# A pre-norm block with linear attention and a mixture of experts: weights folded through the attention, carried router columns, experts with stationary weights

## The chip, the core and the metric

The kernel runs on one core of one Trainium2 chip. The metric is the device time in microseconds (us) of one execution; the median of three runs is given. All arrays are fp32. TensorE is called PE, VectorE DVE, ScalarE ACT, GpSimd POOL and SyncE SP; each is a queue that runs its instructions strictly in the order written, so an instruction that waits on a semaphore holds up all that stand behind it on its engine.

## The reference, cut to what matters

```python
# x: (4, 1024, 128); 16 heads of 8; 16 experts of 128 -> 2*128 -> 128; shared FFN of 512
n = layernorm(x)
q, k = l2norm_per_head(n @ Wq + bq), l2norm_per_head(n @ Wk + bk)
v = n @ Wv + bv
out = (q @ k.T / S ** sigmoid(m)) @ v          # no softmax, per batch and head
x = x + out @ Wo + bo
h = layernorm(x)
logits = h @ router_w.T                        # 16 experts, top 1
s = sigmoid(top logit)                         # of the chosen expert, else 0
gate, up = split((s * h) @ gate_up[e])
expert = (up * silu(gate)) @ down[e]
shared = silu(h @ shared_gate_w.T) * (h @ shared_up_w.T) @ shared_down_w.T
return x + shared + expert
```

## The kernel before, in words

The 4096 rows are 32 tiles of 128 rows, taken as 8 quads of 4 tiles (`NQ`, `Q`); two quads are one batch (`QB`). Since there is no softmax, attention of a batch is q times a 128x128 matrix: the sum over rows of v^T k, masked to the heads' blocks and multiplied by Wo.

Every engine's program is a list of calls written out by hand, one call per helper and quad (or per shared chunk `n`, 4 per quad, or per expert group `g`, 4 slots of 128 rows each, 12 groups). The lists are different on the five queues and semaphores tie them together; nothing is reordered while it runs.

**Stage one, attention and routing, quads in turn.** PE: `project` (x against q, k and v weights, 384 columns, L1096), `v_by_k` (L1105), `fold_wo` (L1114), `turn_q` (transposes, L1122), `attend` (the bias as a matmul, L1129, x by the identity, L1130, q by the folded matrix, L1135), `turn_h` (L1143), `route` (h against 16 router columns, L1152), `count_before` (how many earlier rows chose each expert). DVE: `stats` (L721, L724), `take` (scales and biases the projection, L758), `head_sums` (L766), `inv_norms` (L771), `h_scales` (L743, L744), `choose` and `place` (the chosen expert of each row and its row in the sorted array, L791 to L811; their temporaries lie in PSUM). ACT: squares, roots, PSUM copies, `norm_h`. POOL: `scale_q` and `scale_v` (L319), `hT_lo` (L329), `count` (L336) and `scatter` (L345): one indirect DMA per tile writes its 128 rows of h, with score and row number, to their places in `x_slots` in DRAM, at most two in flight.

**Shared FFN.** h is split in a high part (rounded to fp32r) and a remainder, `hT_lo`, and each product of it is three fp32r matmuls of 512 columns: `gate_up_shared` (6 matmuls, L1181 to L1183), `silu_shared` on ACT, `act_shared` on DVE (L843), `down_shared` (L1203). 32 chunks; they fill PE between the other work and make the tail.

**Stage two, experts.** When all 32 scatters have landed and `table` (first row and expert of each of the 48 slots, by `slot_rows` and `take_table` on DVE) is there, SP loads the slots, 4 DMAs per group (`load`, L248), 12 groups in turn. Per group: `turn_rows` on PE (L1215), `rows_copy` on ACT (L528), `gate_up_experts` (rows stationary, weights of the expert moving, 4 matmuls of 256 columns, L1226), `score_tanh` on ACT and `score` on DVE, `gate` (four ACT instructions, L536), `gated` (four on DVE, L868), `turn_act` (four transposes of the activations, L1234) and `turned_act` (L877), `down_experts` (L1245), `take_y` (L545), and `send` on POOL (L354): one indirect DMA per slot back to `y_back`, at most three in flight.

**Tail.** When all 48 have landed, SP brings `y_back` in 8 DMAs (L254), `add_shared` (L849) and `add_experts` (L855) on DVE add up, and 8 DMAs write `out` (SP and ACT queues in turn).

Of the kernel before, what the change touches and what calls it, by code (L numbers as in the profile page):

```python
# [7 lines left out]
ALU = mybir.AluOpType  # L8
ACT = mybir.ActivationFunctionType
AX = mybir.AxisListType  # L10
# [8 lines left out]
def build_block(nc, S, x, x_t, w_in, b_in, Wo, bo, m_col_in, router_t, gate_up, down, shared_gate, shared_up,  # L19
                shared_down, out):  # L20
# [6 lines left out]
    _, E, F2 = gate_up.shape  # L27
    F = F2 // 2
# [8 lines left out]
    QKV = 3 * D  # L37
    W = D + 2
    QRING = 2
    RING = 3  # L40
    EPS = 1e-5
    YRING = 12
# [9 lines left out]
    with ExitStack() as ctx:  # L52
# [6 lines left out]
        xres = sb("xres", [P, NT, D])  # L59
# [4 lines left out]
        st1 = sb("st1", [P, NT, 6])  # L64
        mv1 = sb("mv1", [P, NT, 2])
        rs1 = sb("rs1", [P, NT])
        nm2 = sb("nm2", [P, NT])
        st2 = sb("st2", [P, NT, 6])
        mv2 = sb("mv2", [P, NT, 2])
        rs2 = sb("rs2", [P, NT])  # L70
        w_o = sb("w_o", [P, D])
# [11 lines left out]
        rwT = sb("rwT", [P, E])  # L83
# [7 lines left out]
        s_act = sb("s_act", [P, 2, 512])  # L91

        place_of = sb("place_of", [P, Q, E])
        near = sb("near", [P, Q])
        hot = sb("hot", [P, NQ, E, Q])
        incl = sb("incl", [P, 2, E, Q], BF16)
        run_mask = sb("run_mask", [P, E, Q])
# [19 lines left out]
        with ExitStack() as attention:  # L117
            def sb_a(name, shape, dt=F32):
                return attention.enter_context(nc.sbuf_tensor(name, shape, dt))

            qkv = sb_a("qkv", [P, QRING, Q, QKV])
            sq = sb_a("sq", [P, Q, 2 * D])
            xT = sb_a("xT", [P, T])
            qT = sb_a("qT", [P, RING, Q * P])
            ss = sb_a("ss", [P, 2, Q, 2 * HEADS])
            rn = sb_a("rn", [P, 2, Q, 2 * HEADS])
            vkm = sb_a("vkm", [P, 2, D])
            wb = sb_a("wb", [P, 2, D])
            w_qkv = sb_a("w_qkv", [P, D + QKV])
            b_qkv = sb_a("b_qkv", [P, QKV])  # L130
            w_c = sb_a("w_c", [P, QKV])
# [3 lines left out]
            zeros = sb_a("zeros", [P, E, W])  # L135
            w_sh = sb_a("w_sh", [P, 2, SF])
            bo_in = sb_a("bo_in", [2, D])
            bo_top = sb_a("bo_top", [2, D], F32R)
            bo_two = sb_a("bo_two", [P, Q, D], F32R)
            two_col = sb_a("two_col", [2, 1])  # L140
            ones_r = sb_a("ones_r", [P, P], F32R)
# [1330 lines left out]
```

## Time and profile before

| | |
|---|---|
| median of 3 runs | 213.24 us (212.55 to 214.74) |
| the profiled execution | 212.35 us |
| its span, first to last instruction | 210.6 us |
| PE busy | 185.7 us, 88% |
| DVE busy | 137.5 us, 65% |
| POOL busy | 111.8 us, 53% |
| ACT busy | 103.1 us, 49% |
| mean DMA rate over the span | 102 GB/s |

The span is what the trace covers; 1.75 us of the execution's own time lie around it. Busy shares are means over very different stages, so they are read with the strips of the page (40 slices of 5.3 us) and with the timelines. A matmul of fp32 is two PE instructions in the trace; their recorded durations overlap, so work is better measured from start to start.

### The profile page before, as it was taken

The page shows a single profiled execution, that of the slowest core. Times are in us where ns is not written, and L with a number is a line of the kernel's source. Part 1 is how long each engine was busy: PE and PEld are TensorE (multiplying, and loading weights), DVE is VectorE, ACT ScalarE, POOL GpSimd, SP SyncE. Part 2 cuts the span into 40 slices and gives each one's busy share as a digit, 9 for nine tenths or more (in the row PEclk, how much of TensorE's full clock was granted, in tenths as well). Part 3 has the DMA queues.
Part 4 walks back from the last instruction along what each step waited for, and adds up shares of the span by engine and source line. Part 5 has one row for each costly group of instructions (what it writes and reads, how often), then busy time and mean ns, then how long its engine had stood idle before and what let it go on. Part 6 is the DMA issues. An engine that isn't in the chain of part 4 may idle for free.

```text
span 210.6 us, 3716 instructions
## 1 busy us (share of the span) xinstructions
PE 185.7 (88%) x1110; PEld 152.0 (72%) x1110; DVE 137.5 (65%) x430; ACT 103.1 (49%) x234; POOL 111.8 (53%) x142
## 2 busy tenths in 40 slices
PE   0797698988989699889779999999999999979992
PEld 0344566766668477778568999889999889869882
DVE  4789999999999979667443455454545233237553
ACT  3434474967564798943323666565634322312320
POOL 7003405348779786757800177767777767750000
PEclk9999999999999999999999999999999999999998
DMA  6999993001100011111134456511111100048143
GB/s 171 302 390 269 174 413 134 2 0 38 40 30 25 26 38 41 51 40 51 41 85 106 114 136 154 143 43 43 42 40 38 50 31 0 0 135 311 56 165 133
DMA packets 17606, 21.58 MB, mean 102 GB/s; under 512 B 3224, under 2 KB 11679, under 8 KB 17332
## 3 DMA queue, kind: packets, MB, share of 16 engines
q1 hardware_dynamic: 13872, 15.73, 26.3%
q0 software_dynamic: 2560, 4.24, 6.1%
q10 hardware_dynamic: 1156, 1.39, 1.9%
q8 instruction: 9, 0.15, 0.3%
q14 instruction: 9, 0.07, 0.1%
HBM read 13.95 MB, written 8.44 MB: 106 GB/s over the span
## 4 chain that ended last, share of the span: by engine, by line
PE 35%; DVE 31%; DMA 12%; POOL 10%; issue 8%; ACT 2%; POOLq 1%; ACTq 0%; DVEq 0%
PE quad_banks L1226 8%; DVE qkv L758 7%; DMA y_back<-yg,xg 7%; PE bank L1203 7%; POOL y_back L354 7%; DVE ss L766 4%; DVE st L721 4%; PE quad_banks L1181 3%; PE bank L1245 3%; PE quad_banks L1183 3%; PE quad_banks L1182 3%; DMA x_slots<-h_rows,pos 3%; POOL x_slots L345 2%; PE bank L1215 2%; PE quad_banks L1096 2%
## 5 line engine op out<-in xcount | busy, mean ns | idle before, releaser
L354 POOL DMA_INDIRECT y_back<-yg,xg x48 | 47.0, 979 | 30.9 <-ACT yg L545 15.2
L843 DVE TENSOR_TENSOR s_act<-quad_banks,sg_act 128x512 f32<-128x512 f32 x32 | 22.1, 689 | 28.9 <-PE bank L1203 16.6
L517 ACT ACTIVATE sg_act<-quad_banks 128x512 f32<-128x512 f32 x32 | 19.1, 598 | 44.5 <-PE quad_banks L1183 44.4
L345 POOL DMA_INDIRECT x_slots<-h_rows,pos x32 | 31.6, 988 | 11.8 <-issue 6.9
L1203 PEld LDWEIGHTS bank<-sdT,s_act 128*128 128x128 f32 x256 | 31.8, 191 | 1.8
L1203 PE MATMUL bank<-sdT,s_act 128*128 128x128 f32 x256 | 32.8, 276 | 0.0
L319 POOL TENSOR_TENSOR qkv<-qkv,rn 128x512 f32<-128x512 f32 x16 | 17.1, 1081 | 26.6 <-DVE rn L771 26.5
L1096 PE MATMUL quad_banks<-w_c,xT 128*128 128x384 f32 x64 | 25.0, 525 | 2.1 <-DVE qkv L758 1.3
L1226 PE MATMUL quad_banks<-w_gu,xgT 128*128 x96 | 22.9, 381 | 0.8 <-ACT xgT L528 0.8
L868 DVE SCALAR_TENSOR_TENSOR e_act<-quad_banks,esc,eg_act 128x128 f32<-128x128 f32 x48 | 13.5, 344 | 10.6 <-ACT eg_act L536 10.6
L1096 PEld LDWEIGHTS quad_banks<-w_c,xT 128*128 128x128 f32 x64 | 11.9, 204 | 11.0 <-issue 3.6
L1226 PEld LDWEIGHTS quad_banks<-w_gu,xgT 128*128 128x128 f32 x96 | 17.3, 190 | 2.9 <-issue 1.0
L536 ACT ACTIVATE eg_act<-quad_banks,esc 128x128 f32<-128x128 f32 x48 | 13.7, 371 | 9.3 <-PE quad_banks L1226 8.6
L758 DVE SCALAR_TENSOR_TENSOR qkv<-quad_banks,rs,b_qkv 128x384 f32<-128x384 f32 x32 | 17.6, 601 | 0.5 <-PE quad_banks L1096 0.5
L1181 PE MATMUL quad_banks<-hT,sgT 128*128 128x512 f32 x32 | 14.8, 462 | 3.3 <-DVE s_act L843 1.9
L877 DVE COPY e_actT<-bank 128x512 f32<-128x512 f32 x12 | 8.3, 690 | 13.0 <-PE bank L1234 13.0
L721 DVE BATCH_NORM_STATS2 st<-xres 128x6 f32<-128x128 f32 x64 | 13.7, 277 | 0.3 <-DMA xres<-L_attn_x 0.3
L473 ACT ACTIVATE h_rows<-xres,nm,rs 128x128 f32<-128x128 f32 x32 | 13.2, 484 | 1.0 <-DVE nm L744 1.0
L1245 PE MATMUL bank<-w_dn,e_actT 128*128 x96 | 12.7, 275 | 0.0
L1183 PE MATMUL quad_banks<-hT,sgT 128*128 128x512 f32 x32 | 12.7, 395 | 0.0
L1182 PE MATMUL quad_banks<-hT,suT 128*128 128x512 f32 x32 | 12.7, 395 | 0.0
L1245 PEld LDWEIGHTS bank<-w_dn,e_actT 128*128 128x128 f32 x96 | 12.3, 191 | 0.5
(141 smaller groups left out, 348.0 us busy)
## 6 DMA issues: line engine op xcount, KB each, us to landing
xg<-x_slots SPq DMA_DIRECT2D x48, 65.0 KB, 1.9
xT<-x_t SPq DMA_DIRECT2D x8, 256.0 KB, 7.1
xres<-L_attn_x SPq DMA_DIRECT2D x8, 256.0 KB, 7.2
w_gu<-gate_up SPq DMA_DIRECT2D x1, 2048.0 KB, 14.4
h_rows<-y_back SPq DMA_DIRECT2D x8, 256.0 KB, 5.4
x_slots<-zeros SPq DMA_DIRECT2D x1, 1040.0 KB, 16.4
w_dn<-down SPq DMA_DIRECT2D x1, 1024.0 KB, 16.4
out<-xres SPq DMA_DIRECT2D x4, 256.0 KB, 2.0
```

Source lines behind the costliest of these rows:

```text
L345: g.indirect_dma_start(out=x_slots, out_offset=bass.IndirectOffsetOnAxis(ap=pos[:, t:t + 1], axis=0), in_=h_rows[:, t, :], in_offset=None) ...
L354: nc.gpsimd.indirect_dma_start(out=y_back, out_offset=bass.IndirectOffsetOnAxis(ap=xg[:, n, D + 1:D + 2].bitcast(I32), axis=0), in_=yg[:, ...
L517: a.activation(sg_act[:, n % 2], pair[:, 2 * (n % 2)], ACT.Silu).then_inc(s_silu, 1)
L721: last = v.bn_stats(st[:, t, :], xres[:, t, :])
L758: last = v.scalar_tensor_tensor(out=qkv[:, c % QRING, j, :], in0=pair[:, j, 0:QKV], scalar=rs1[:, t:t + 1], in1=b_qkv[:], op0=ALU.mult, op ...
L843: v.tensor_tensor(s_act[:, n % 2], pair[:, 2 * (n % 2) + 1], sg_act[:, n % 2], ALU.mult).then_inc(s_act_rdy, 1)
L1096: last = te.matmul(pair[:, j, 0:QKV], xT[:, P * (Q * c + j):P * (Q * c + j + 1)], w_c[:], start=True, stop=True)
L1181: te.matmul(to, lhs[:, 0], rhs[:, 0], start=True, stop=False)
L1182: te.matmul(to, lhs[:, 0], rhs[:, 1], start=False, stop=False)
L1203: last = te.matmul(Y_BANK[c][:, here], s_act[:, n % 2, here], sdT[:, D * k:D * k + D], start=(k == 0 and j == 0), stop=(k == KC - 1 and j ...
L1226: mm = te.matmul(gate_up_banks(g % 2)[:, j, :], xgT[:, g % 2, P * j:P * j + P], gu_cols[:, bass.ds(held[g][j] * 2, F2)], start=True, stop= ...
L1245: mm = te.matmul(ps_yg[:, here], e_actT[:, g % 2, here], dn_cols[:, bass.ds(cols[j], D)], start=True, stop=True)
```

## The change

1. No product for v. `project` multiplies by q, k and the 16 router columns only (272 columns). `gram` multiplies the scaled k by the raw rows of x with two more columns (128 + 2); `turn_g` and `v_of_g` bring Wv and bv in afterwards, once per batch. `scale_k` takes the place of `scale_v`, and its factor takes one more DVE multiply (`scale_inv`).
2. Router logits are carried: x's part is kept by `keep` (from the projection), the attention's part comes as 16 more columns of `attend` (`wo_x` has 144 columns), `sum_logits` adds the two. `route` is gone. The temporaries of the choice (`lg`, `far`, `offs`, `rank`) lie in SBUF, and the one helper is cut in ten calls with their own places in the list. `scatter` waits also for the score and for `norm_h`.
3. `attend` transposes x with bo added by ACT (`bias_x`) instead of the bias matmul and the identity product, in two halves per quad.
4. Statistics of two tiles are taken by one instruction over interleaved rows, so that even and odd elements are the two tiles; the aggregation is gone.
5. Experts: DVE multiplies the loaded rows by the score (`scale_rows`), ACT copies each slot's gate/up weights to a fixed place (`take_weights`), PE holds the weights stationary with the rows moving (8 matmuls of 128 columns), so that activations come out transposed: `turn_act` and `turned_act` are gone, `gate` and `gated` are one instruction each.
6. Remainders `hT_lo` are all on POOL, six of the eight now ahead of the last scatters.
7. All lists are written anew.

```diff
-            def attend(c, after=None):
...
-                te.matmul(ps_qy[:], ones_r[:], bo_two[:].rearrange("p j d -> p (j d)"), start=True, stop=False)
-                te.matmul(ps_qy[:], ident[:], xres[:, Q * c:Q * c + Q, :].rearrange("p j d -> p (j d)"), start=False,
-                          stop=False)
+            def attend(c, h, after=None):
...
+                for j in (0, 1):
+                    te.matmul(ps_y[:, YW * j:YW * j + D], xT_b[:, c % XRING, P * (2 * h + j):P * (2 * h + j + 1)], ident[:],
+                              start=(j == 0), stop=False, is_transpose=True, skip_group_check=True)
...
+            def gram(c, after=None):
...
+                    last = te.matmul(ps_v[:, 0:W], qk[:, c % QRING, j, D:QK], xres[:, Q * c + j, :],
+                                     start=(h == 0 and j == 0), stop=(h == QB - 1 and j == Q - 1))
...
+            def gate_up_experts(g, after=None):
+                pe.wait_ge(w_rdy, g + 1)
+                pe.wait_ge(xgT_sb, g + 1)
+                free(after)
+                for half in (0, 1):
+                    for j in range(Q):
+                        here = slice(P * j, P * j + P)
+                        mm = te.matmul(pair[:, 2 * (g % 2) + half, here], w_now[:, (g * Q + j) % WRING, F * half:F * half + F],
+                                       xgT[:, g % 2, here], start=True, stop=True)
...
+            def take_weights(g):
...
+                for j in range(Q):
+                    last = a.copy(w_now[:, (g * Q + j) % WRING], gu_cols[:, bass.ds(first[j] * 2, F2)])
...
             def stats(c, rows, st, done):
+                for n in (0, 1):
+                    last = v.bn_stats(st[:, 2 * c + n, :], by_two(rows, Q * c + 2 * n))
...
+            def below_top(c):
+                need(("top", c))
+                mark(("below", c), v.tensor_tensor(far[:, c % 2], lg[:, c % 2], top[:, quad(c)].unsqueeze(2).broadcast_to([P, Q, E]), ALU.is_lt))
...
+            def scale_rows(g):
+                dve.wait_ge(esc_rdy, g + 1)
...
+                v.tensor_tensor(rows, rows, esc[:, here].unsqueeze(2).broadcast_to([P, Q, D]), ALU.mult).then_inc(xg_rdy, 1)
```

ACT's new list around the first expert groups:

```diff
+            score_tanh(0)
+            silu_shared(11)
+            hT_copy(7)
+            score_tanh(1)
+            hT_hi(7)
+            silu_shared(12)
+            rows_copy(0)
+            score_tanh(2)
+            silu_shared(13)
+            score_tanh(3)
+            gate(0)
+            rows_copy(1)
+            score_tanh(4)
+            take_weights(2)
+            take_y(0)
+            rows_copy(2)
+            score_tanh(5)
+            score_tanh(6)
+            gate(1)
+            take_weights(3)
+            score_tanh(7)
+            rows_copy(3)
+            score_tanh(8)
+            take_y(1)
+            rows_copy(4)
+            score_tanh(9)
+            gate(2)
+            take_weights(4)
+            score_tanh(10)
+            score_tanh(11)
+            gate(3)
+            rows_copy(5)
+            take_y(2)
```

DVE's new list in the same place:

```diff
+            scale_rows(3)
+            gated(0)
...
+            scale_rows(6)
+            gated(1)
...
+            scale_rows(9)
+            gated(2)
...
+            scale_rows(11)
+            gated(3)
```

POOL's new list from the first scatter on, with runs of one call drawn together: scatter 0 to 3, count 1, `hT_lo(0)`, scatter 4 and 5, `scale_k(4)`, scatter 6 and 7, `scale_k(5)`, `scale_q(4)`, `scale_q(5)`, count 2, `hT_lo(1)`, scatter 8, count 3, scatter 9 to 12, `scale_k(6)`, scatter 13 and 14, `scale_q(6)`, count 4, scatter 15, `scale_k(7)`, `scale_q(7)`, scatter 16, count 5, scatter 17 and 18, `hT_lo(2)` to `hT_lo(4)`, scatter 19 and 20, count 6, scatter 21 and 22, `hT_lo(5)`, scatter 23 to 26, count 7, scatter 27 to 31, `hT_lo(6)`, `hT_lo(7)`, then the 48 sends. PE's new list puts 13 `gate_up_shared` and 9 `down_shared` ahead of `turn_rows(0)` (before: 10 and 8).

## Rows read from the trace of the kernel before

**Rows 1.** The page's strips: busy tenths of two engines in 40 slices.
```profile
PE   0797698988989699889779999999999999979992
DVE  4789999999999979667443455454545233237553
```

**Rows 2.** DVE groups by line: busy us, mean ns, idle before and releaser.
```profile
L758 DVE SCALAR_TENSOR_TENSOR qkv<-quad_banks,rs,b_qkv 128x384 f32<-128x384 f32 x32 | 17.6, 601 | 0.5 <-PE quad_banks L1096 0.5
L721 DVE BATCH_NORM_STATS2 st<-xres 128x6 f32<-128x128 f32 x64 | 13.7, 277 | 0.3 <-DMA xres<-L_attn_x 0.3
...
L766 DVE TENSOR_REDUCE ss<-sq 128x128 f32<-128x1024 f32 x8 | 9.6, 1200 | 0.2 <-ACT sq L489 0.2
...
L771 DVE RECIPROCAL rn<-rn 128x128 f32<-128x128 f32 x8 | 7.5, 934 | 0.0
L724 DVE BATCH_NORM_AGGREGATE mv<-st 128x2 f32<-128x6 f32 x64 | 6.1, 157 | 0.6
```

**Rows 3.** DVE timeline, stage one: start us, us, line, what.
```profile
11.04 1.14 DVE L758 SCALAR_TENSOR_TENSOR qkv<-quad_banks,rs,b_qkv 128x384 f32<-128x384 f32 x2 [0.18 <-PE quad_banks L1096]
...
45.58 0.16 DVE L811 TENSOR_TENSOR pos<-bank,near 128x4 int32<-128x4 f32 x1
```

**Rows 4.** POOL timeline, stage one: first and last scatters, and two others.
```profile
46.67 1.19 POOL L345 DMA_INDIRECT x_slots<-h_rows,pos  x1 [0.63 <-issue]
...
55.92 2.12 POOL L319 TENSOR_TENSOR qkv<-qkv,rn 128x512 f32<-128x512 f32 x2
...
60.49 1.29 POOL L329 TENSOR_TENSOR hT<-hT_full,hT 128x512 fp32r<-128x512 f32 x1
...
79.96 0.98 POOL L345 DMA_INDIRECT x_slots<-h_rows,pos  x1 [0.58 <-DVE pos L811]
...
101.95 0.96 POOL L345 DMA_INDIRECT x_slots<-h_rows,pos  x1 [0.31 <-issue]
```

**Rows 5.** PE groups by line, of products that go or shrink.
```profile
L1096 PE MATMUL quad_banks<-w_c,xT 128*128 128x384 f32 x64 | 25.0, 525 | 2.1 <-DVE qkv L758 1.3 <-ACT w_c L451 0.7
...
L1130 PE MATMUL bank<-xres,ident 128*128 128x512 f32 x16 | 8.2, 591 | 0.0
L1152 PE MATMUL bank<-rwT,hT_full 128*128 128x16 f32 x64 | 8.0, 257 | 0.2 <-ACT hT_full L479 0.2
```

**Rows 6.** The chain that ended last, expert stage: start us, us, what.
```profile
118.98 1.73 PE quad_banks L1226 x8
120.71 0.44 PE bank L1234 x4
```

**Rows 7.** PE timeline: two shared chunks in a row, and the first expert rows.
```profile
97.29 0.48 PE L1181 MATMUL quad_banks<-hT,sgT 128*128 128x512 f32 x1
...
99.59 0.48 PE L1181 MATMUL quad_banks<-hT,sgT 128*128 128x512 f32 x1
...
109.34 0.60 PE L1215 MATMUL bank<-ident,xg 128*128 128x128 f32 x4
```

**Rows 8.** SP's queue: the 48 slot loads, from the first issue to the last.
```profile
105.79 30.36 SPq L248 DMA_DIRECT2D xg<-x_slots  x48
```

**Rows 9.** ACT group, a copy of 512 columns in the expert stage.
```profile
L528 ACT COPY xgT<-bank 128x512 f32<-128x512 f32 x12 | 7.2, 597 | 8.6 <-PE bank L1215 8.6
```

**Rows 10.** DVE instructions with two inputs in SBUF: ns min/median/max; one of them in time.
```profile
L744 DVE SCALAR_TENSOR_TENSOR nm<-mv,rs x8: 161/162/1572, 35.7 to 85.9; 128x4 f32<-128x4 f32 x8
...
L784 DVE TENSOR_TENSOR suT<-w_sh,suT x1: 2265/2265/2265, 64.6 to 64.6; 128x512 fp32r<-128x512 f32 x1
...
57.47 0.59 DVE L744 SCALAR_TENSOR_TENSOR nm<-mv,rs 128x4 f32<-128x4 f32 x1
```

**Rows 11.** The end: the first and last send, and DVE's last instruction.
```profile
120.39 1.01 POOL L354 DMA_INDIRECT y_back<-yg,xg  x1 [14.94 <-ACT yg L545]
...
183.67 0.98 POOL L354 DMA_INDIRECT y_back<-yg,xg  x1 [0.30 <-issue]
...
207.43 0.69 DVE L855 TENSOR_TENSOR xres<-xres,h_rows 128x512 f32<-128x512 f32 x1
```

More of the change, by code:

```diff
@@ L408, in _ @@
             scatter(25)
-            count(6)
             scatter(26)
@@ L927, in _ @@
+            x_stats(5)
+            keep(2)
+            x_stats(6)
+            inv_norms(2)
+            take(3, 0)
+            gram_out(0)
+            x_stats(7)
+            scale_inv(2)
+            take(3, 1)
+            mask_vk(0)
+            keep(3)
+            weights_lo(0)
+            weights_lo(1)
+            head_sums(3)
+            take(4, 0)
+            x_scales(5)
+            inv_norms(3)
+            sum_logits(0)
             x1_stats(0)
-            x_scales(5)
-            head_sums(3)
@@ L930, in _ @@
-            x_stats(6)
-            inv_norms(3)
+            top_logit(0)
+            scale_inv(3)
+            below_top(0)
             h_scales(0)
+            places(0)
+            nearest(0)
+            choose(0)
+            run_count(0)
+            score_row(0)
+            keep(4)
+            h_shift(0)
+            take(4, 1)
             x1_stats(1)
-            take(4, 0)
-            take(4, 1)
-            x_stats(7)
+            add_base(0)
+            own_only(0)
+            ranks(0)
@@ L937, in _ @@
             h_scales(1)
-            mask_vk(1)
-            weights_lo(0)
-            head_sums(4)
-            choose(0)
+            put(0)
+            sum_logits(1)
+            gram_out(1)
+            h_shift(1)
+            top_logit(1)
+            below_top(1)
+            places(1)
+            nearest(1)
+            take(5, 0)
+            head_sums(4)
+            mask_vk(1)
+            choose(1)
+            run_count(1)
+            take(5, 1)
+            add_base(1)
+            own_only(1)
@@ L942, in _ @@
+            keep(5)
+            ranks(1)
+            put(1)
+            score_row(1)
+            x_scales(6)
+            x_scales(7)
+            head_sums(5)
             inv_norms(4)
-            place(0)
-            take(5, 0)
-            x_scales(6)
-            take(5, 1)
+            scale_inv(4)
+            inv_norms(5)
+            sum_logits(2)
             x1_stats(2)
-            choose(1)
+            top_logit(2)
+            below_top(2)
             h_scales(2)
-            head_sums(5)
@@ L951, in _ @@
-            place(1)
+            score_row(2)
+            h_shift(2)
+            scale_inv(5)
             take(6, 0)
-            inv_norms(5)
+            take(6, 1)
+            places(2)
+            nearest(2)
+            sum_logits(3)
             x1_stats(3)
-            x_scales(7)
-            take(6, 1)
-            h_scales(3)
-            choose(2)
-            head_sums(6)
-            mask_vk(2)
-            place(2)
+            choose(2)
+            top_logit(3)
+            run_count(2)
@@ L962, in _ @@
+            gram_out(2)
+            below_top(3)
+            add_base(2)
+            own_only(2)
+            ranks(2)
+            put(2)
+            places(3)
+            h_scales(3)
+            h_shift(3)
+            nearest(3)
+            mask_vk(2)
+            choose(3)
+            run_count(3)
+            head_sums(6)
+            add_base(3)
+            own_only(3)
+            ranks(3)
+            put(3)
+            keep(6)
+            score_row(3)
             inv_norms(6)
+            scale_inv(6)
```

1451 lines of the change are left out of this document (816 added, 635 removed).

## The prediction, on record before the result was seen

> **What bounds the kernel now.** I read the strips first [rows 1]: DVE is full in the first third, PE from the middle to the end. So it is two kernels. In stage one a quad costs what its chain on DVE costs [rows 2, 3]; in stage two PE runs without a gap from the first expert rows at 109.34 [rows 7]. Then I read the queues that no busy share shows. POOL issues its first scatter at 46.67 and its last at 101.95 [rows 4]; the slot loads start at 105.79, once all scatters have landed [rows 8], and the first rows reach PE at 109.34, 6.4 us after the last scatter's end (102.9). SP needs 30.36 us for the 48 loads [rows 8]: 2.53 us per group. Nobody waits for that now, since no engine's list takes a group's rows much before it needs them. The sends run from 120.39 to 183.67, 1.28 us apart once they are steady [rows 11]. The end is PE at 206.6 and 4 us of DVE and output behind it.
>
> I call T the time when group 0's rows are in. Before, T is 109.3 and the rest takes 210.6 - 109.3 = 101.3 us. I forecast the two separately.
>
> **What PE saves, and why most of it is not on the path.** `project` has 272 columns instead of 384: 32 matmuls, about a fifth to a quarter of 25.0 us, 6 us [rows 5]. `route` goes: 7 us of 8.0 recorded. Identity product and bias product become four transposes per quad: 5 us (from 8.2, with the bias). All that is 18 us less in stage one, where DVE and POOL set the pace, and where PE already waits. It only lets chunks of the shared FFN move ahead. `turn_act` goes from stage two: 12 x 0.44 [rows 6] = 5.3 us. Stationary weights cost 8 matmuls of 128 columns, by the 0.44 for four half-price transposes 1.78 us, against 1.73: +0.6 in all.
>
> **DVE in stage one.** The first position is written at 45.74 [rows 3]. By then the list holds five quads of `take`: a tile costs 601 ns recorded, 0.52 from start to start, and 128 columns less save 0.13 at the slope that the 128-column ones share: 20 x 0.13 = 2.6. Ten quad statistics lose their aggregation and half of their instructions: 1.19 to 0.70 each, 5.0. One `head_sums` (1.12) and one `inv_norms` (0.85) move behind it: 2.0 [rows 2]. Added are `keep`, `scale_inv`, the subtraction in `x_scales`, the copy of `wo_x`, one weight remainder and the sum of logits: 3.6. The first `take` comes later: ACT now does `bias_x(0)`, which waits for the last of its loads, and `bias_x(1)` before `wc_copy`, and the weights' product waits for the bias load; I put it at 12.6 against 11.04 [rows 3], +1.6. Sum 45.7 - 9.6 + 3.6 + 1.6 = 41.3, with 1 us of waits on the longer chain from `gram` to `wb` 42.3. The choice itself keeps its count. Carried down the list, DVE alone would place the last quad near 87, against 96 now.
>
> **POOL in stage one.** This is the step that I think decides. Behind the first scatter POOL has 31 steps of 1.28 and a last 0.96, 8 scalings at 1.0, six `hT_lo` at 1.2 and seven counts at 0.1 (durations by [rows 4], less the gap that they fill): 39.7 + 1.0 + 8.0 + 7.2 + 0.7 = 56.6. In before two of those remainders stood there and there were 4 us of idle time. Scatters also wait for the landing of the one two before: the last sixteen took (101.95 - 79.96) / 15 = 1.47 each [rows 4]; I take 3 us for that, 1 for late inputs. 42.6 + 56.6 + 4 = 103.2. So the nine microseconds that DVE gains end on POOL, and the last scatter ends where it ended. Bounds: no wait at all, 98.5 to 99; waits as dense as now over all scatters, 106.
>
> **A price for the port.** The route's temporaries move from PSUM to SBUF, so that some eleven DVE instructions per quad (sum, comparison, places, choice, scan, own, position, score, `scale_inv`, shift, subtraction) read two SBUF tensors. Such instructions exist now: the shift L744, with 161 ns as a rule, took 1572 once, and 590 at 57.47, ending at 58.06 where POOL's scaling from 55.92 ends (58.04); the weight remainder L784 took 2265, beside `hT_lo` [rows 10, 4]. So DVE waits for a POOL operation that is under way. There are 24 of POOL's in stage one, each 1.1 to 1.3 us. Before the first position I count two or three such meetings, 1.5 us: last scatter 104.7, T = 104.7 + 6.4 = 111.1. Bounds 0 and 5 us.
> The Trainium skill (SBUF — State Buffer, Who interferes with whom) says that GpSimd and a DVE instruction with two SBUF inputs take turns on one port, the later one blocked for the whole instruction; the trace agrees in these three rows. Were every one of the 24 met half way, by that rule DVE would lose some 9 to 13 us; that is a rival below.
>
> **Stage two.** PE's work from T on: 12 groups at 0.44 + 1.78 + 0.89 (four down products, twice the four transposes) = 3.11 make 37.3; a gate/up and a down chunk together take 99.59 - 97.29 = 2.30 [rows 7], 19 pairs and four more downs 47.2: 84.5. Before it was 94.2 by the same count, and ran in 97.3. But the new lists read the loads ahead: ACT has `score_tanh(3)` before `gate(0)`, (6) before `gate(1)`, (9) before `gate(2)`, (11) before `gate(3)`, and DVE `scale_rows` of the same groups before `gated`. Each waits for its group's four loads, and these come every 2.53 us [rows 8], so group 11's at T + 27.5. Behind that: tanh, score, scaled rows, `gated(3)` 1.7, so that `down_experts(3)` starts at T + 29.2. Until then PE can do 6 `turn_rows`, 5 `gate_up_experts`, 3 `down_experts`, one gate/up and three down chunks, 18.3 us: it idles for 10.9 us, though shared chunks are there, since its list has none in that place. Left behind it are 84.5 - 18.3 = 66.2: PE ends at T + 95.4, with 1.5 for ACT (four weight copies and a register load per group, 1.3 to 1.5 us by half of the 597 ns [rows 9]; up to `gate(8)` ACT has 14.7 and PE 15.2) at T + 96.9. The last output is one DVE sum shorter: 3.2. So T + 100.1, against T + 101.3 now. If the loads did not bind it would be T + 1.5 + 84.5 + 2 + 3.2 = T + 91.
> Sends: the first at T + 12; group 2 is taken only behind `gate(3)`, at T + 29.3, and from there ten groups at 5.14 end at T + 80.7. Results come back 5 to 11 us later; `add_experts(0)`, with `act_shared(27)` behind it, fits at T + 86, just when PE wants it. It costs nothing as long as PE is that late; without PE's gap the sends would end the kernel 1 to 2 us earlier than this.
>
> **Sum.** 111.1 + 100.1 = 211.2 of span, 212.9 with the 1.75 around it, against 212.35 of the profiled execution: +0.6. That execution lies 0.9 under the median of 213.24, which would make it 213.8; I keep 212.8, since each of my prices for POOL's waits stands above its lower bound: no change that can be measured. (About 1% is what a measurement of this kernel can tell: below 211.1 is faster, over 215.4 slower.)
>
> **Rivals.**
> - *Faster, 29%.* Either POOL's queue is not full (landing waits hidden under the scalings, no port waits before the first position): last scatter at 100 to 101, T near 107, 107 + 100.1 + 1.75 = 208.8; or the loads come faster than now, since nothing else uses the rings then, or fall less in ACT's way: each 10% of their 2.53 is 2.8 us, and without that gap at all and T as forecast it is 111.1 + 91 + 1.75 = 203.9, where the sends (T + 12 + 61.7 + 18) hold it at 204.6. For it: the same instructions, 0.5 us apart at the start of the burst. Against it: the 30.36 us is measured with the same queue and list. 204.5 to 210.5.
> - *Slower, 27%.* The port. If DVE meets most of POOL's 24 operations, with 9 to 13 us of waits, it no longer has the 9 us in hand: `put(7)` falls at 99 to 103 and the four last scatters behind it end at 105 to 108, T = 112 to 114.5, 214 to 216.5; and where POOL is full at the same time and waits for late scalings, both add, 216 to 220. It decides from about 9 us of such waits. For it, three of some ten such instructions of now that are not scans were hit; against it, none of the eight scans, which also read two.
> - *The statistics or the port-free parts cost more than counted, so the redesign does nothing at all*, 2%: same.
> - The forecast's own case, 42%: 210.6 to 215.8.
>
> **How the numbers follow.** Faster 0.29 and 0.05 of the forecast's own: 0.34. Slower 0.27 and 0.02: 0.29. Same 0.37. The range reaches from 205.5 to 219, and leaves a tenth at each side.
>
> **What would show it.** POOL without gaps between the first and the last scatter, the last ending at 102 to 106; DVE done with the last position well ahead of scatter 28. PE's busy share falling to about 60% for 28 us behind T, `score_tanh` and `scale_rows` waiting on the slot loads, `down_experts(3)` at T + 29. PE work near 20 us less and idle time near 20 us more. DVE's `below_top` and its like at 230 ns as a rule, with some over 1 us. I am wrong if T lies under 107 (POOL's count is wrong), if the loads take under 22 us, or if DVE still places a quad every 9 us.

## The result, and the profile after

The changed kernel takes 230.45 us (median of 4 runs, 228.5 to 231.02) against 213.65 of the kernel before in the same job: ratio 1.077, 95% interval 1.068 to 1.086. It is slower, outside the range that ended at 219, and past the slower rival's 216 to 220. The profiled execution spans 229.2 us, 18.0 more than the 211.2 of my sum. Of these, 11.1 lie ahead of T (122.2 instead of 111.1) and 6.9 behind it (107.0 instead of 100.1).

The strips of the page, busy tenths and granted clock in 40 slices, answer to [rows 1].
```profile
PE   0364859959548969998896786879999999994394
...
DVE  3239789999998798568734634632231422240591
...
PEclk9999779997995997999999999999999999999589
```
PE is full only from two thirds on, has a hole just before the end, and its clock falls to half of full speed for parts of the first half. Before, the windows from 20 to 110 show a granted clock of 1.00.

**The start.** ACT's and DVE's timelines (start, us, what; in brackets the idle time before it and who ended it) answer to [rows 3].
```profile
8.87 0.29 ACT L506 ACTIVATE m_tmp<-m_col,zero_col 128x1 f32<-128x1 f32 x1 [4.76 <-DMA m_col<-m_of_column]
...
12.84 0.47 ACT L515 COPY w_c<-quad_banks 128x400 f32<-128x400 f32 x1
```
```profile
15.69 0.88 DVE L902 SCALAR_TENSOR_TENSOR qk<-quad_banks,rs,b_all 128x256 f32<-128x256 f32 x2 [1.85 <-PE quad_banks L1425]
...
48.04 0.16 DVE L1005 TENSOR_TENSOR pos<-rank,near 128x4 int32<-128x4 f32 x1
```
The load of m, a column of 128 numbers, was first on ACT's queue and is now third: it lands 7.1 us after its issue instead of 3.5, and ACT waits 4.76 us for it. The copy of the weights stands behind it in ACT's list. The first `take` is at 15.69, not at 12.6.

**DVE between the first and the last position.** Busy us of PE, PEld, DVE, ACT and POOL in that stretch, then the clock: before, and after.
```profile
45.60:95.80 50.20, 44.61 (x277) 34.95 (x276) 43.37 (x157) 33.89 (x70) 38.58 (x43) 1.00 0.11 36
```
```profile
48.00:107.80 59.80, 48.01 (x273) 39.53 (x271) 50.95 (x156) 45.63 (x96) 42.73 (x46) 0.89 0.09 29
```
DVE has as many instructions as before, 156 against 157, and is busy 7.6 us longer. Its groups in that stretch (count, busy us, mean ns, idle before) say where most of it is:
```profile
L964 DVE SCALAR_TENSOR_TENSOR far<-far,place_of 128x64 f32<-128x64 f32 x7 | 3.8, 547 | 0.1
...
L952 DVE TENSOR_TENSOR lg<-x,kept 128x64 f32<-128x64 f32 x7 | 3.2, 464 | 0.1
...
L960 DVE TENSOR_TENSOR far<-lg,top 128x64 f32<-128x64 f32 x7 | 2.9, 420 | 0.2
```
The same 64 columns, with an operand in PSUM, took 233 ns before. These means hide single long ones. Three of them, each with what GpSimd runs at the time:
```profile
53.80 1.81 DVE L1005 TENSOR_TENSOR pos<-rank,near 128x4 int32<-128x4 f32 x1
54.32 1.26 POOL L352 TENSOR_TENSOR hT<-hT_full,hT 128x512 fp32r<-128x512 f32 x1
63.03 2.46 DVE L964 SCALAR_TENSOR_TENSOR far<-far,place_of 128x64 f32<-128x64 f32 x1
62.27 3.13 POOL L342 TENSOR_TENSOR qk<-qk,rn 128x512 f32<-128x512 f32 x3
85.44 1.61 DVE L960 TENSOR_TENSOR far<-lg,top 128x64 f32<-128x64 f32 x1
84.85 2.11 POOL L342 TENSOR_TENSOR qk<-qk,rn 128x512 f32<-128x512 f32 x2
```
Each ends within 0.1 us of the end of GpSimd's instruction, or of the last in a row of them (55.61 and 55.58, 65.49 and 65.40, 87.05 and 86.96). There are nine such cases up to the last position, two of them ahead of the first, and together they took 9.8 us more than such instructions take otherwise (0.16 or 0.23 us). In the kernel before there were three, of 3.4 us.

**POOL**, its first and last scatter, for [rows 4], and SP's slot loads, for [rows 8]:
```profile
49.12 1.18 POOL L370 DMA_INDIRECT x_slots<-h_rows,pos  x1 [3.17 <-DVE pos L1005]
...
116.34 0.96 POOL L370 DMA_INDIRECT x_slots<-h_rows,pos  x1 [1.14 <-DMA x_slots<-h_rows,pos]
```
```profile
118.85 28.73 SPq L271 DMA_DIRECT2D xg<-x_slots  x48
```
**Stage two.** ACT's waits between 120 and 152 (total, times, longest), and the product that I had named:
```profile
ACT half_tanh L606 <- DMA xg<-x_slots: 16.1, 11, 2.7
```
```profile
151.01 1.15 PE L1570 MATMUL bank<-w_dn,e_act 128*128 x8 [1.69 <-DVE e_act L1081]
```
`down_experts(3)` starts at T + 28.8. This part came as forecast.

**The sends and the tail** answer to [rows 11].
```profile
203.69 0.98 POOL L378 DMA_INDIRECT y_back<-hT_full,xg  x1 [0.30 <-issue]
207.44 0.97 POOL L378 DMA_INDIRECT y_back<-hT_full,xg  x1 [2.76 <-DMA y_back<-hT_full,xg]
208.72 0.98 POOL L378 DMA_INDIRECT y_back<-hT_full,xg  x1 [0.30 <-issue]
```
```profile
214.16 0.69 DVE L1061 TENSOR_TENSOR hT_full<-x,h_rows 128x512 f32<-128x512 f32 x1 [8.34 <-DMA h_rows<-y_back]
214.77 0.68 DVE L1037 TENSOR_TENSOR s_act<-quad_banks,sg_act 128x512 f32<-128x512 f32 x1
...
226.02 0.69 DVE L1052 TENSOR_TENSOR hT_full<-bank,x 128x512 f32<-128x512 f32 x1 [2.25 <-PE bank L1537]
```
```profile
PE quad_banks L1512 <- DVE s_act L1037: 6.6, 1, 6.6
```
The last send ends at 209.7, T + 87.5. `add_experts(0)` waits for what it brings, `act_shared(27)` stands behind it in DVE's list, and PE waits 6.6 us for that. Before, the last send ended 25.9 us ahead of the kernel's end, 21.9 us ahead of PE's, and nobody waited for it.

### The profile page after: what moved, and what is told of

Read it like the earlier page. It is cut to its first block, busy times and chain, and to the rows that moved or that the text cites. A ratio compares the mean times of both kernels' runs of the same rounds, so it can differ in the third digit from the quotient of the medians.

```text
span 229.2 us, 3735 instructions
## 1 busy us (share of the span) xinstructions
PE 179.8 (78%) x1120; PEld 154.2 (67%) x1120; DVE 132.3 (58%) x341; ACT 120.7 (53%) x268; POOL 111.7 (49%) x142
## 4 chain that ended last, share of the span: by engine, by line
PE 29%; DVE 18%; DMA 13%; POOL 13%; issue 13%; SPq 10%; ACT 2%; ACTq 1%; POOLq 0%; DVEq 0%
SPq L271 8%; POOL y_back L378 6%; PE quad_banks L1425 6%; DMA x_slots<-h_rows,pos 6%; PE bank L1537 4%; PE quad_banks L1557 4%; POOL x_slots L370 4%; DMA wo_all<-wo_in 3%; PE bank L1570 3%; DVE qk L902 3%; PE quad_banks L1512 2%; DMA y_back<-hT_full,xg 2%; PE quad_banks L1514 2%; PE quad_banks L1513 2%; DVE st L866 2%
## 5 line engine op out<-in xcount | busy, mean ns | idle before, releaser
L378 POOL DMA_INDIRECT y_back<-hT_full,xg x48 | 47.3, 985 | 35.4 <-ACT hT_full L640 15.6
L342 POOL TENSOR_TENSOR qk<-qk,rn 128x512 f32<-128x512 f32 x16 | 17.1, 1077 | 31.2 <-DVE rn L922 28.4
L1425 PE MATMUL quad_banks<-w_c,xT 128*128 128x272 f32 x64 | 22.5, 504 | 6.8 <-ACT w_c L515 5.7
L1557 PE MATMUL quad_banks<-xgT,w_now 128*128 128x128 f32 x192 | 23.3, 276 | 1.7 <-DVE s_act L1037 1.1
L1557 PEld LDWEIGHTS quad_banks<-xgT,w_now 128*128 128x128 f32 x192 | 22.3, 192 | 2.4 <-issue 2.3
L1425 PEld LDWEIGHTS quad_banks<-w_c,xT 128*128 128x128 f32 x64 | 15.0, 249 | 10.9 <-ACT w_c L515 6.0
L902 DVE SCALAR_TENSOR_TENSOR qk<-quad_banks,rs,b_all 128x256 f32<-128x256 f32 x32 | 13.8, 474 | 6.4 <-PE quad_banks L1425 6.3
L622 ACT COPY w_now<-w_gu 128x256 f32 x48 | 15.7, 408 | 0.8 <-issue 0.8
L1570 PE MATMUL bank<-w_dn,e_act 128*128 x96 | 13.1, 279 | 3.5 <-DVE e_act L1081 3.2
L1570 PEld LDWEIGHTS bank<-w_dn,e_act 128*128 128x128 f32 x96 | 11.8, 191 | 4.4 <-issue 4.1
L546 ACT ACTIVATE h_rows<-x,nm,rs 128x128 f32<-128x128 f32 x32 | 13.2, 483 | 1.7 <-DVE nm L888 1.6
```

Of the source, the lines that this page charges most:

```text
L378: g.indirect_dma_start(out=y_back, out_offset=bass.IndirectOffsetOnAxis(ap=xg[:, n, D + 1:D + 2].bitcast(I32), axis=0), in_=yg[:, n // Q % ...
L902: last = v.scalar_tensor_tensor(out=qk[:, c % QRING, j, :], in0=pair[:, j, 0:QK], scalar=rs1[:, t:t + 1], in1=b_all[:, 0:QK], op0=ALU.mult ...
L1425: last = te.matmul(pair[:, j, 0:PROJ], xT[:, P * (Q * c + j):P * (Q * c + j + 1)], w_c[:, 0:PROJ], start=True, stop=True)
L1557: mm = te.matmul(pair[:, 2 * (g % 2) + half, here], w_now[:, (g * Q + j) % WRING, F * half:F * half + F], xgT[:, g % 2, here], start=True, ...
L1570: mm = te.matmul(E_BANK[g][:, here], e_act[:, g % 2, here], dn_cols[:, bass.ds(cols[j], D)], start=True, stop=True)
```

## Experiments

My theory from these rows: the redesign's arithmetic does what it should, and five orders of the lists that came with it, together with the port that DVE shares with GpSimd, make it slower. The main rival: PE's clock and the port, which no order mends. Ratios are to the kernel before in the same job (median 214.4 us for e1 to e4, 214.8 for e5 to e8, 213.0 for e9 to e12), in brackets their 95% intervals; the changed kernel's is 1.077 [1.068 to 1.086].

One trace per run also has its spread. e1_jit, e2_sends and e7_adds leave the lists ahead of T as they are in the changed kernel, and over these four traces the first scatter starts at 47.40 to 49.12, the last at 112.99 to 116.34, and T is 118.8 to 122.2. A difference ahead of T is read against that.

### e1_jit: stage two's reads in time
```
-score_tanh(2) .. score_tanh(11) ahead of gate(0), gate(1), gate(2), gate(3)
+t3 y0 r2 g1 w3 t4 r3 t5 y1 r4 g2 w4 t6 g3 r5 y2 w5 t7 ... (t score_tanh, g gate, w take_weights)
 and DVE: scale_rows(2) and (3) around gated(0), ... scale_rows(9) behind gated(6)
```

> The changed kernel, with only the calls of score_tanh, score and scale_rows moved back in ACT's and DVE's lists, so that each stands about two groups ahead of its use and no gate or gated stands behind a far later group's load. Theory (the pace of the slot loads holds ACT and DVE, and so PE, for 29 us behind the first rows): down_experts(3) starts at T + 18 to 21 instead of T + 28.8, the last send ends 6 to 8 us earlier, the time falls by 6 to 9 us to 221 to 224. Rival (PE waits there for the weight copies or for its own turn_rows, whatever the order of the scores): down_experts(3) moves by less than 3 us and the time by less than 2.

225.32 us, 1.055 [1.042 to 1.068], just over my 221 to 224; the interval only touches that of the changed kernel. ACT's waits for the loads fall from 16.1 to 4.1 us, and `down_experts(3)` comes at T + 22.0 instead of T + 28.8 (T + 18 to 21 expected). But PE still waits 6.9 us for `act_shared(27)`: the last send ends at 202.4, T + 80.9, and PE, now earlier, meets it again. So the wait behind T costs some 5 us here, less than the 10.9 that I took PE to idle.

### e2_sends: the sends in order
```
 send_one(10)
+send_one(11)
 send_one(12)
 send_one(13)
-send_one(11)
-send_one(16)
 send_one(14)
 ...
-send_one(43)   (it stood behind 45, now behind 42)
```

> The changed kernel with the 48 sends in the order of their slots instead of 12, 13, 11, 16, 14, 15 and so on. Each send waits for the landing of the one three slots before, so out of order some wait for a send issued just before. Theory (that order is why 40 sends take 58.2 us, 1.46 each, against 1.28): 1.28 to 1.32 each, the last send 4 to 6 us earlier, and since DVE waits for the results with the last chunks behind it the time falls by as much, to 225 to 227. Rival (the landings themselves are slower than before, or ACT hands the groups over late): under 1.5 us.

224.39 us, 1.051 [1.039 to 1.063]. The last four sends:
```profile
195.96 0.98 POOL L378 DMA_INDIRECT y_back<-hT_full,xg  x1 [0.30 <-issue]
197.24 0.98 POOL L378 DMA_INDIRECT y_back<-hT_full,xg  x1 [0.30 <-issue]
198.52 0.98 POOL L378 DMA_INDIRECT y_back<-hT_full,xg  x1 [0.30 <-issue]
199.81 0.98 POOL L378 DMA_INDIRECT y_back<-hT_full,xg  x1 [0.30 <-issue]
```
A send waits for the landing of the third before it by number. Out of order that is one just issued: in the changed kernel `send_one(46)` waits 2.76 us for `send_one(43)`, the row at 207.44. From the ninth send on, the waits above the usual 0.30 sum to 7.2 us there (12 of 39) and to 0.7 us here (2 of 39), and the pitch is 1.30 us instead of 1.47. The last send ends at T + 82.0 instead of T + 87.5. The theory holds: this one list costs about 6 us, as much as the reading ahead. The span of this trace is 9.2 us shorter, but 3.4 of that lie ahead of T, where nothing was changed.

### e3_start: the small load first
```
+act.dma_start(m_col[:], m_col_in)        (first on ACT's queue, was third)
+wc_copy()                                (behind mask_exp2, was behind bias_x(1))
```

> The changed kernel with the load of m first on ACT's queue again and wc_copy right behind the two exponentials, ahead of bias_x and x_std. Theory (the first take comes 4.6 us later than before since m lands at 8.9 and wc_copy stands behind bias_x, and nothing later makes this up): take(0, 0) at 11.5 to 12.5 instead of 15.7, first scatter 3 us earlier, time 2.5 to 4 us less. Rival (POOL and the scatters' landings set the end of routing anyway): first rows in at the same time within 1 us, time within 1 us.

228.98 us (225.44 to 229.93): the spread is wider than the 2.5 to 4 us that I expected, so a gain in time is not shown. In the trace the first pair of `take` begins at 13.45 (11.5 to 12.5 expected; 15.37 to 15.86 in the four traces with the old order) and the first scatter is at 43.76, 3.6 to 5.4 earlier than in those four:
```profile
43.76 1.19 POOL L370 DMA_INDIRECT x_slots<-h_rows,pos  x1 [3.19 <-DVE pos L1005]
```
The last scatter is at 111.80, T is 117.7, 1.1 to 4.5 earlier than in the four, and the last send ends at T + 88.3. That fits a start that is on the path, but one trace doesn't show how much of it reaches T.

### e4_noread: GpSimd reads nothing for q and k
```
-g.tensor_tensor(v, v, r, ALU.mult)
+g.memset(v, 1.0)   (twice)
```
q and k are not scaled here, so rows go to other experts and stage two isn't comparable; two memsets take the time of the product. The eight remainders `hT_lo` still read.

> The changed kernel with POOL's sixteen scalings of q and k replaced by two memsets each of the same tile, about as long in all but reading nothing from SBUF; q and k are then not scaled, which leaves the routing of rows to experts different. Theory (a DVE instruction with two inputs in SBUF stands still while POOL's elementwise operation runs): the DVE instructions of 0.9 to 2.5 us on 64 or fewer elements at 43.7, 53.8, 59.0, 63.0, 77.6, 81.1 and 85.4 are gone except beside hT_lo, together some 7 to 9 us of DVE, and the first rows come in 3 to 7 us earlier. Rival (they are a minor part, the landings of the scatters set the pace): the long instructions go, but the first rows come less than 2 us earlier. Third case (the length has nothing to do with what POOL reads): the long ones stay.

226.04 us, 1.054 [1.043 to 1.066]. DVE and its groups in the same stretch:
```profile
45.30:101.40 56.10, 45.97 (x276) 37.40 (x274) 44.78 (x156) 45.91 (x96) 42.55 (x54) 0.94 0.10 31
```
```profile
L968 DVE SCALAR_TENSOR_TENSOR far<-far,place_of 128x64 f32<-128x64 f32 x7 | 1.6, 226 | 0.1
L964 DVE TENSOR_TENSOR far<-lg,top 128x64 f32<-128x64 f32 x7 | 1.6, 224 | 0.2
L956 DVE TENSOR_TENSOR lg<-x,kept 128x64 f32<-128x64 f32 x7 | 1.5, 214 | 0.6 <-ACT x L545 0.5
```
GpSimd is as busy as before (42.55 us), DVE is busy for 44.78 instead of 50.95 us with the same 156 instructions, and the three groups are back at 214 to 226 ns. The port is shown, and the scalings' share of it in that stretch is 6.2 us. GpSimd's memsets, which only write, don't lengthen DVE's instructions. Beside two remainders, which still read, two positions are long here too (1.79 and 0.83 us instead of 0.16): 2.3 us more that this run leaves in. The last scatter starts at 109.78, earlier by 6.6 than in the changed kernel's trace and by 3.2 than in that of e2_sends.

### e5_lo_late: three remainders off GpSimd's path
```
-hT_lo(3) hT_lo(4)  (ahead of scatter(19))   -hT_lo(5)  (ahead of scatter(23))
+hT_lo(3) hT_lo(4) hT_lo(5)                  (behind scatter(31))
```

> The changed kernel with three of GpSimd's remainders, hT_lo(3), hT_lo(4) and hT_lo(5), moved behind its last scatter; nothing is left out. In the changed kernel they stand at 92.15 (three in a row, 3.75 us with hT_lo(2)) and 102.91 (1.31 us), before scatters. Theory GpSimd (the remainders are on its path to the last scatter, as the forecast's term had it): 3 x 1.25 = 3.8 us come off, the last scatter starts at 112.5 to 113.5 instead of 116.34, and the time is 225.5 to 228. Rival theory DVE and the landings (GpSimd waits 6.4 us for pos and 9.0 us for the landing of an earlier scatter, so its own work is cover): the last scatter starts within 1 us of 116.34, and the time is that of the changed kernel, 229 to 232. Where the shared products 12 to 20 then wait for the remainders, TensorE loses up to 3 us ahead of the rows, which would show in its idle time at 100 to 120.

229.05 us, 1.061 [1.051 to 1.071]. First and last position fall where they did (47.91 and 107.68 for 48.04 and 107.75), and the last scatter starts at 112.93, 3.4 us earlier, as the theory GpSimd has it:
```profile
112.93 0.96 POOL L370 DMA_INDIRECT x_slots<-h_rows,pos  x1 [0.30 <-DMA x_slots<-h_rows,pos]
```
That is 5.3 us behind the last position, against 7.3 to 9.1 in the four traces with the remainders in front, so GpSimd was the bound there for the last 2 to 4 us only. The time moves by about 1.4: the interval overlaps that of the changed kernel. The last send ends at 208.3 instead of 209.7: T is 119.4, 2.8 earlier, and from T to the last send's end it takes 88.9 us instead of 87.5. The sends are still out of order there.

### e6_ahead: the kernel before, reading ahead
```
 score_tanh(0) score_tanh(1)
+score_tanh(2) score_tanh(3)
 gate(0)
+score_tanh(4) score_tanh(5) score_tanh(6)
 gate(1)
 ... (and score_tanh(11) ahead of gate(3); DVE's scores alike)
```

> The kernel before, with one part of the change alone: its scores are read as far ahead as the new lists have them (score_tanh(11) ahead of gate(3) on ACT, scale_rows(11) ahead of gated(3) on DVE); nothing is left out. Theory of the forecast's step on stage two: the slot rows of group 11 land 28 us after those of group 0 (11 x 2.53), so the fourth gate can't start before T + 28, TensorE idles 6 to 10 us between T + 12 and T + 29, down_experts(3) comes at T + 28 to T + 29.5 (before T + 18, 127.1 less 109.3), and the time is 218 to 224. Rival theory (the list costs nothing by itself, since the kernel before has shared products left to fill in, and its last send has 6 us to spare: 25.9 us from the last send to the end against 19.5 in the changed kernel): 213 to 216.

224.26 us, 1.041 [1.034 to 1.049]. One part of the change, done alone, costs over half of the whole loss.
```profile
ACT half_tanh L522 <- DMA xg<-x_slots: 15.4, 10, 3.3
```
```profile
120.46 1.12 PE L1234 MATMUL bank<-ident,e_act 128*128 128x128 f32 x4 [3.02 <-DVE e_act L868]
...
127.55 0.65 PE L1234 MATMUL bank<-ident,e_act 128*128 128x128 f32 x4 [1.06 <-DVE e_act L868]
...
135.58 1.11 PE L1234 MATMUL bank<-ident,e_act 128*128 128x128 f32 x4 [3.95 <-DVE e_act L868]
```
The fourth down product begins at 144.14 instead of 130.14, 33.7 us behind the first expert rows on PE and not 28 to 29.5. The rival, that shared products fill in, is wrong: they are in PE's list, but behind what waits. The granted clock falls too, to 0.69 from 130 to 140, so the gap is paid twice.

### e7_adds: the adds behind the last product
```
-add_experts(0) (ahead of act_shared(27)) ... add_experts(6), add_shared(6) (ahead of act_shared(30))
+add_experts(0) ... add_experts(6), add_shared(6), add_experts(7) (behind act_shared(31))
```

> The changed kernel with DVE's add_experts(0) to (6) moved behind its act_shared(31), so that no shared product waits for a row that is sent back; nothing is left out. Theory (the sends end too late, at T + 87.5, and TensorE waits for them 6.6 us through act_shared(27)): the wait goes, TensorE's last products end some 6 us earlier, and what is left is the loads of y_back and the adds, which end at about 219 + 2.4 with the stores behind them: 223 to 226. Rival theory (the tail is set by the sends whatever stands in front: last send 209.7, loads land until 217.3, adds and stores some 5 us): 227 to 230. Neither moves the last send: it ends at 209 to 210.

232.74 us, 1.088 [1.078 to 1.097]. Both theories missed it. The wait for `act_shared(27)` goes, and another comes: the shared products of all quads share one bank now, `add_shared(6)` frees it, and I had put it behind seven adds. PE waits 6.5 us for it at 219.75, as long as for `act_shared(27)` before. e8_all has this fault too:
```profile
205.56 6.36 PE L1537 MATMUL bank<-sdT,s_act 128*128 128x128 f32 x32 [6.51 <-DVE hT_full L1052]
```

### e8_all and e9_tail: all orders together
e8_all has the edits of e1, e2, e3, e5 and e7. e9_tail mends its tail:
```
-SHARED_FIRST = [0, 1, 2, 3, 4, 5]
+SHARED_FIRST = [0, 1, 2, 3, 4, 5, 6]
-down_shared(28, after=(fin, 7))
+down_shared(28, after=(y_free, 7))       (and add_shared(6) ahead of act_shared(30))
```

> The changed kernel with five of its orders changed together: m_col loaded first and w_c's copy behind the masks (first scatter 5.4 us earlier), scores read in time instead of ahead (TensorE's 10.9 us idle after the rows gone), the sends in order (1.30 us each instead of 1.455), three remainders behind the last scatter, and the adds behind the last act_shared; nothing is left out. Theory that these orders, and not the redesign's arithmetic, made the kernel slower, with effects that add up because they lie one behind another: T at 113 to 117 instead of 122.2, last send at T + 72 to 76, TensorE's idle after T under 3 us, and the time 203 to 210, under the kernel before. Rival theory (TensorE's clock and the port take what is left: it runs at 0.83 for much of 20 to 90, and DVE's long reads stay): 210 to 216, no better than the kernel before.

> e8_all with its tail mended: chunk 6 adds the shared product first, as chunks 0 to 5 do, so that the one bank of the shared products comes free behind add_shared(6), which stands ahead of act_shared(30), and not behind all the adds; the eight add_experts stand behind act_shared(31). Nothing is left out. In e8_all the last 32 down matmuls waited 6.5 us for that bank (205.56) and then ran in 6.36 us instead of 4.2. Theory (that wait was made by my move, and e7_adds shows the same 5.6 us): they run from about 199.4, the last add is at 205 to 206, the span is 208 to 210 against 215.1, and the time 210 to 213.5, at or just under the kernel before (214.8 in the last job). Rival theory (the sends set the end: last send 192.6, and 19.5 us from there as in the changed kernel make 212): span 211 to 213, time 214 to 217.

e8_all: 218.48 us, 1.019 [1.012 to 1.027], over the ranges of both theories, with the fault of e7_adds in it. e9_tail: 211.32 us, 0.988 [0.981 to 0.995]. The end of e9_tail on PE, then on DVE:
```profile
201.71 3.73 PE L1537 MATMUL bank<-sdT,s_act 128*128 128x128 f32 x32
```
```profile
203.14 4.29 DVE L1061 TENSOR_TENSOR hT_full<-x,h_rows 128x512 f32<-128x512 f32 x7
...
208.14 0.69 DVE L1052 TENSOR_TENSOR hT_full<-bank,x 128x512 f32<-128x512 f32 x1
```
The same 32 products take 3.73 us at a granted clock of 1.00 instead of 6.36 at 0.58: without the gap the clock stays up. With the orders mended, the redesign is faster than the kernel before by 1.2%, though T is 117.4 against 109.3. Behind T it takes 93.9 us; before it was 101.3. So the five orders together account for the loss of time, and the rival (clock and port alone hold it at or above the kernel before) is refuted, if narrowly: the interval ends 0.5% under the kernel before. Clock and port are still there in this kernel, and T is still 8.1 us later than before; it is stage two and the tail that pay for that.

### e10_ring, e11_fill, e12_both: what is left ahead of T
```
-scat = [sem("scat0"), sem("scat1")]      +four of them (e10, e12)
+fill(20) behind turn_g(1), fill(28) behind turn_q(4), ... 121 products nobody reads (e11, e12)
```

> e9_tail with the scatters on four semaphores in turn instead of two, so that a scatter waits for the landing of the fourth before it, not of the second; nothing is left out. Theory landings (GpSimd waits 9.0 us for landings in the changed kernel, 12 times, and 4.6 us, 11 times, in e8_all, with 2.3 us from issue to landing and 1.29 us between issues): these waits go, the last scatter starts 3 to 5 us earlier than in e9_tail (108.1 in e8_all), and the time is 2 to 4 us under that of e9_tail. Rival theory (the queue takes the scatters no faster, or DVE's pos(7) is what sets the last four): the landings get longer in step, the last scatter starts within 1.5 us of e9_tail's, and the time within 1 us.

> e9_tail with 121 matmuls of 128 columns whose output nobody reads, put in seven places of TensorE's list where it waits between 43 and 83 us (20, 9, 16, 18, 28, 14 and 16 of them, about 0.07 us each, so 0.6 to 2 us a place); nothing is left out. Theory clock (TensorE falls to its lower level behind these waits, granted clock 0.71 in 60:70 of e8_all, and runs the eight projections at 68.39 in 3.27 us instead of 2.07, on the path to DVE): the granted clock stays at 0.95 to 1.00 from 40 to 90, the projections take 2.1 us, the last scatter starts 1.5 to 3 us earlier, and the time is 1 to 3 us under e9_tail's. Rival theory (the low clock hits work that others hide): the clock rises and the time is that of e9_tail within 1 us, or up to 2 us above it where a filler holds up the matmul behind it.

> e9_tail with both the ring of four semaphores and the 121 filling matmuls; nothing is left out. If landings and clock are each on the path to the last scatter, the last scatter starts at 101 to 104 and the time is 3 to 7 us under e9_tail's, 205 to 209, below the kernel before by 2 to 4 per cent. If DVE's pos(7) sets it, only the filler's gain is left, and the time is 0 to 3 us under e9_tail's.

212.0 us, 0.989 [0.980 to 0.997]; 212.24 us, 0.994 [0.989 to 0.998]; 210.59 us, 0.987 [0.983 to 0.992]. All three intervals overlap that of e9_tail, and e12_both is 0.7 us under it where I had 3 to 7 if landings and clock were both on the path. The waits ahead of the scatters of e10_ring:
```profile
  DVE pos L1005: 7.5, 4
  issue: 6.8, 26
  ACT h_rows L546: 1.4, 1
  DMA x_slots<-h_rows,pos: 0.3, 1
```
In e9_tail the landings are 6.1 us of these and pos 6.4, and from the start of the first to that of the last scatter it is 65.2 us there and 65.6 here. The landing waits hid behind DVE's positions; the rival holds. With the fillers PE's clock is full from 60 to 70 (e9_tail, then e11_fill):
```profile
60.00:70.00 10.00, 6.17 (x34) 0.78 0.05 16
```
```profile
60.00:70.00 10.00, 8.21 (x80) 1.00 0.07 21
```
The eight projections take 2.07 us instead of 3.08, and from first to last scatter it is 62.5 instead of 65.2 us in the two profiles; e8_all, with e9_tail's lists ahead of T, has 63.9. The medians don't show it. Whether it is a gain of under 1% stays open.

## Why the prediction was wrong

The recorded sum fails in four terms.

1. *DVE in stage one* ("DVE alone would place the last quad near 87"). It placed it at 107.75, a quad every 8.5 us against 7.2 before. I counted savings per tile up to the first position and carried them down the whole list. But between the first and the last position DVE has as many instructions as before, and without the scalings' reads it is busy as long: 44.78 us (e4_noread) against 43.37. In that stretch `take` and the statistics do save 4.3 us (9.7 against 14.0). Against that stand 4.3 us of work that the new list moved in, one more `head_sums` and `inv_norms`, which I had booked as a gain ahead of the first position, and three more `act_shared` in e4_noread, and 5.3 us of new instructions (the sum of logits, the score, `scale_inv`, `keep` and `gram_out`, which takes the product for `turn_g`). These are sums of durations, which overlap a little. The nine microseconds in hand never were. POOL, which I held for the bound, bound only the end (e5_lo_late). Of its 6.4 us of waits for positions 3.3 lie behind its first scatter; my 3 us for landings were 9.0, but with the landing waits gone (e10_ring) nothing moved.
2. *The port.* I took 1.5 us ahead of the first position, and there it was 1.1, in two meetings. Behind the first position I put it at nothing, since the reserve of point 1 would cover it. There seven meetings cost 8.7 us, 6.2 of them beside the scalings (e4_noread). With 9.8 us in all the rival's "9 to 13" was right in place and size, but I had it decide only "from about 9 us", set against that reserve. I also misread two of my three rows. DVE's long instructions at 75.14 and 64.58 began before the ones of GpSimd beside them:
```profile
65.00 1.29 POOL L329 TENSOR_TENSOR hT<-hT_full,hT 128x512 fp32r<-128x512 f32 x1
75.60 1.09 POOL L319 TENSOR_TENSOR qkv<-qkv,rn 128x512 f32<-128x512 f32 x1
```
So the prediction's sentence that the later one is blocked, and that the trace agrees in these three rows, fits only one of them by the trace's starts. In each of the long cases here DVE was held until GpSimd had ended, whoever began first, and GpSimd's scalings kept their 1.08 us.
3. *The start.* 15.69 instead of 12.6: I saw `bias_x` in front of `wc_copy` and not the load of m as third on ACT's queue. e3_start has the first scatter 3.6 to 5.4 us earlier.
4. *The sends and the tail.* I let ten groups run at 5.14 us each, the steady pitch of before, in a list whose order I had not checked against its three semaphores: T + 80.7 became T + 87.5 (e2_sends takes 5.5 of the 6.8 back). And "fits at T + 86, just when PE wants it" had no margin: PE waited 6.6 us.

In numbers, ahead of T: start +3.1, the way from there to the first scatter +3.4, from the first scatter's start to the last one's end 68.2 instead of 62.1, +6.1, and the rows 1.5 sooner behind it: 11.1.

How much of the 6.1 is port and how much clock, one more trace helps to say. Here is the stretch between the first and the last position in e2_sends, whose lists are the changed kernel's there:
```profile
47.30:105.70 58.40, 45.73 (x272) 37.33 (x271) 50.56 (x155) 45.73 (x96) 44.18 (x48) 0.94 0.09 31
```
Its granted clock happened to be 0.94, that of e4_noread, which needs 56.1 us; the other three need 59.7 to 60.3 at 0.89. So I estimate, from single traces, 2.3 us of the stretch for the scalings' reads and 1.3 to 1.9 for the clock between 0.89 and 0.94. DVE's 6.2 us shorten the stretch by far less: without them it waits longer for PE and ACT (9.1 us in e4_noread, 6.4 in the changed kernel). The kernel before needs 50.2, and no run with the changed lists comes under 56; what the rest is, none isolates.

Right were: stage two's reading ahead (T + 28.8 for T + 29.2; PE was busy for 22.4 of the 30 us from 120 on, so it idled for 7.6 where I had 10.9; e6_ahead shows the price in the kernel before), the loads' pace (28.73 us for 48), and PE's work behind T: the sum without the gap was T + 91, and e9_tail has T + 93.9. Off the path, PE's busy time fell by 5.9 us (185.7 to 179.8) and not by near 20. I missed in all of it that PE falls to its lower clock when it waits, as in e6_ahead. The kernel before ran at 1.00 in the traces that I had, so my sum had no term for it.

## What to carry to other kernels

Before counting what a redesign saves, read its hand-written lists against what they wait for: a list that reads a load three groups ahead of its use, or sends out of the order of its semaphores, cost 5 to 6 us each here. A gain that comes from moving work behind a point is paid again behind it.
